# A recurrence whose new state is one scan of three elements, and a search whose sums stand inside the next count's products

## The chip, the cores and the metric

The kernel runs on one core of one Trainium2 chip. The metric is device time in microseconds, the median of several executions. Five engines work side by side and wait for each other through semaphores: PE (matrix products), DVE (elementwise, reductions, scans), ACT (activations), POOL (a second elementwise engine) and SP (which here issues transfers).

## The reference, cut to what matters

There are 4 batches of 512 rows and 512 features. Four layers are added to `x` one after the other: a top-5120 mask, attention, a GRU over the 512 rows, and a resampling. Two of them are touched:

```
# layer 0, for each batch: the 5120 largest of 512*512 values become 1, all others 0
_, idx = jax.lax.top_k(flat, k)
out = jnp.zeros((g, n * n)).at[rows, idx].set(1.0)

# layer 2: one GRU cell, 512 steps one after the other, D = 512, 4 batches
gh = h @ W_hh + b_hh
r = jax.nn.sigmoid(i_r + h_r)
z = jax.nn.sigmoid(i_z + h_z)
n = jnp.tanh(i_n + r * h_n)
h_new = (1.0 - z) * n + z * h
```

## The kernel before, in words

The program of each engine is written out by hand, in order, with explicit waits; there is no scheduler. What an engine does next is the next instruction of its own program, and it stands until that one's semaphores are reached.

**The search (layer 0).** The 5120th largest value of each batch is found bit by bit. DVE makes a 0/1 mask of 128x2048 elements (`dve_mask`; L992 for the 15 bits of the high half, L1008 and L1005 for the 16 of the low half, L998 for one count between them), PE adds the mask up with 16 matmuls against ones (`pe_count`, L1492), ACT copies the 128 partial sums (`act_search`, L557), PE adds these over the partitions with one more matmul (L1495), and ACT takes the sign of the count against a limit (`act_way`, L580) and moves the bound (`act_bound`, L591), for which the next mask of the same batch waits. The four batches take turns, so count n+4 needs the result of count n. There are 132 counts. The masks of the four batches have buffers of their own.

**The recurrence (layer 2).** The state has 512 features, 4 chunks of 128. Chunks 0 and 1 are half A, chunks 2 and 3 half B. A step on PE is twelve units (`GRU_UNITS`), each named by the half that is read, the half that is written and the gate: `AAr AAz AAn ABr BAr BAz BAn BBr ABz BBz ABn BBn`. A unit is 8 matmuls (L1790): two chunks written, two read, and two parts of the weights, high and low in fp16. The state too stands in two fp16 parts, `parts[parity][half]`, which are read as the moving operand, five copies of 4 batches x 2 parts, 40 columns. The units that read B wait for `lowB`, those that read A for `lowA`.

The result of a half goes round the engines like this. DVE adds the products of r (`dve_r_sum`, L1400) and z (`dve_z_sum`, L1407) out of PSUM into `rz`. ACT makes r (`act_sigmoid_r`, L822, into `mix`) and z (`act_sigmoid_z`, L829). DVE's scan `dve_n_line` (L1415) forms the argument of the tanh, `act_tanh` (L836) writes n into `add`. DVE makes `keep` = (1 - z) scaled (`dve_keep`, L1423), POOL makes z h (`pool_zh`, L497) into the second element of `add`. Then two scans over pairs (n, z h) with the factors (0, keep) give keep n + z h: once rounded to fp16 into `parts` (`dve_high`, L1432) and once in fp32 into `line` (`dve_line`, L1439). `dve_low` (L1448) writes the rounding error as the low part. POOL copies the line into the history (`pool_state`, L504). A scan runs along the free dimension as state = factor * state + addend, and a factor 0 starts it anew.

The order on DVE within a step is: r sum A, z sum A, n line A, r sum B, keep A, high A, line A, z sum B, low A, n line B, keep B, high B, line B, low B. Beside the steps PE has side work after the last unit, in half a group per step (`SIDE`): 8 matmuls of 128 columns for the next inputs' gates (L1723) or 4 in fp32 for output rows (L1750; 96 of the 512 steps). In the first 96 steps DVE and POOL also build the resampling table (`dve_sampling_job`, and two additions on POOL, L486 and L488, in 16 of these steps).

Of the kernel before, what the change touches and what calls it, by code (L numbers as in the profile page):

```python
# [14 lines left out]
P = 128  # L15
# [42 lines left out]
rsumA zsumA nlineA rsigA zsigA tanhA keepA zhA highA lineA lowA stateA putA  # L58
rsumB zsumB nlineB rsigB zsigB tanhB keepB zhB highB lineB lowB stateB putB
# [78 lines left out]
class Kernel:  # L138
# [39 lines left out]
    def layout(self):  # L178
# [38 lines left out]
        self.minus_h_scale = small("minus_h_scale", 1)  # L217
# [80 lines left out]
        self.parts = [[small(f"parts{parity}{half}", 2, B, 2, dtype=FP16) for half in "AB"] for parity in range(2)]  # L298
        self.rz = [small(f"rz{h}", 2, 2, B) for h in "AB"]
        self.z = [small(f"z{h}", 2, B) for h in "AB"]  # L300
# [146 lines left out]
def pool_keys(e, k, b, t):  # L447
# [3 lines left out]
    if n == 0:  # L451
        e.wait_ge(s["prepared"], 11)
# [12 lines left out]
def pool_gru(e, k):  # L465
    s = k.sem
    for half in range(2):
        e.memset(k.mix[half][:], 1.0).then_inc(s["gru_ready"], 1)
        e.memset(k.keep[half][:], 0.0).then_inc(s["gru_ready"], 1)
    e.wait_ge(s["gru_ready"], 4)  # L470
    for half in range(2):
        e.memset(k.mix[half][:, :, :, 0], 0.0).then_inc(s["gru_ready"], 1)
# [18 lines left out]
def pool_zh(e, k, st, half):  # L491
    s = k.sem
    h = "AB"[half]
    e.wait_ge(s[f"zsig{h}"], st + 1)
    if st:
        e.wait_ge(s[f"line{h}"], st)
    e.tensor_tensor(k.add[half][:, :, :, 1], k.z[half][:], k.line[half][:, :, :, 1], ALU.mult).then_inc(s[f"zh{h}"], 1)  # L497


def pool_state(e, k, st, half):  # L500
    s = k.sem
    h = "AB"[half]
    e.wait_ge(s[f"line{h}"], st + 1)
    e.tensor_copy(k.state[:, st + 1, 2 * half:2 * half + 2], k.line[half][:, :, :, 1]).then_inc(s[f"state{h}"], 1)  # L504
# [59 lines left out]
def act_way(e, k, n):  # L564
# [3 lines left out]
    count = k.bank(b, 4)[:, 2:3]  # L568
# [48 lines left out]
def act_columns(e, k, b):  # L617
    s = k.sem
    if b == 0:
        e.wait_ge(s["prepared"], 16)  # L620
# [158 lines left out]
def act_gru(e, k):  # L779
    s = k.sem  # L780
    e.wait_ge(s["hh_scale"], 7)
    unscale = act_register(e, "act_unscale", k.gate_unscale)
    e.wait_ge(s["gru_first"], 17)
# [12 lines left out]
    for st in range(S):  # L796
        q, ss = divmod(st, STEPS_PER_CHUNK)
        act_sigmoid_r(e, k, st, 0, unscale)
        act_sigmoid_z(e, k, st, 0, unscale)
# [4 lines left out]
        act_sigmoid_z(e, k, st, 1, unscale)  # L804
# [20 lines left out]
def act_sigmoid_z(e, k, st, half, unscale):  # L825
# [1010 lines left out]
```

## Time and profile before

| | |
|---|---|
| median of 3 runs | 2473.27 us (2469.03 to 2474.37) |
| the profiled execution's own time | 2475.3 us |
| its span | 2473.6 us |
| PE busy | 2243.5 us (91%) |
| weight loads of PE | 1912.7 us (77%) |
| DVE busy | 1854.6 us (75%) |
| ACT busy | 1295.0 us (52%) |
| POOL busy | 532.7 us (22%) |
| instructions | 139634 |

The span is the time from the first to the last instruction of the profiled execution; busy time is the union of an engine's instructions. Matmuls are pipelined, so their rows overlap and a busy PE need not be at its peak.

### The profile page before, as it was taken

How to read it: one execution, taken by the hardware profiler on the slowest of the kernel's cores; microseconds unless marked ns; L12 is line 12 of the kernel's file. 1: busy time of each engine (PE TensorE's matmuls, PEld its weight loads, DVE VectorE, ACT ScalarE, POOL GpSimd, SP SyncE). 2: the span in 40 equal slices, each digit the busy share in tenths (PEclk: the TensorE clock that was granted, in tenths of full speed). 3: DMA queues.
4: the chain of work that ended last, by engine and by line, in shares of the span. 5: the costliest groups of instructions: out<-in, count | busy, mean ns of one | idle time of the engine just before them, and what ended most of it. 6: DMA issues, size and time to landing. Idle time of an engine off the chain costs nothing.

```text
span 2473.6 us, 139634 instructions
## 1 busy us (share of the span) xinstructions
PE 2243.5 (91%) x58517; PEld 1912.7 (77%) x58517; DVE 1854.6 (75%) x8525; ACT 1295.0 (52%) x5693; POOL 532.7 (22%) x2223
## 2 busy tenths in 40 slices
PE   2668899898987899999999999999999999999998
PEld 2564454555544598988999999999999999999996
DVE  7876877868679588877787777777777768777775
ACT  5564856848557444444445454444444445444443
POOL 1001011020113323333222222222222222222221
PEclk9999899999999999999999999999999999999999
DMA  5000000010010000000000000000000000000000
GB/s 189 3 2 1 1 1 1 2 52 1 1 52 1 18 5 5 5 5 5 5 5 5 9 9 5 9 9 5 9 5 9 9 5 9 9 5 9 5 13 20
DMA packets 8444, 32.08 MB, mean 13 GB/s; under 512 B 836, under 2 KB 904, under 8 KB 7560
## 3 DMA queue, kind: packets, MB, share of 16 engines
q1 hardware_dynamic: 7392, 23.07, 2.5%
q8 instruction: 463, 7.59, 1.3%
q14 instruction: 165, 1.35, 0.2%
q10 hardware_dynamic: 424, 0.07, 0.0%
HBM read 18.94 MB, written 4.19 MB: 9 GB/s over the span
## 4 chain that ended last, share of the span: by engine, by line
PE 48%; DVE 9%; issue 2%; ACT 1%; POOL 1%; DVEq 0%; POOLq 0%
PE psum L1790 41%; PE psum L1723 5%; PE psum L1750 2%; DVE keepB L1423 1%; ACT mixA L822 1%; DVE nlineA L1415 1%; DVE nlineB L1415 1%; DVE rzA L1400 1%; PE psum L1472 1%; DVE keepA L1423 1%; POOL region_rows L486 1%; DVE parts1A L1432 0%; DVE parts0A L1432 0%; DVE lineA L1439 0%; DVEq L1431 0%
## 5 line engine op out<-in xcount | busy, mean ns | idle before, releaser
L1790 PE MATMUL psum<-parts0A,region_w_hh 128*128 128x40 f16 x12288 | 432.5, 179 | 16.2 <-DVE parts0A L1448 10.1
L1790 PE MATMUL psum<-parts1A,region_w_hh 128*128 128x40 f16 x12288 | 433.2, 179 | 15.3 <-DVE parts1A L1448 10.8
L1790 PE MATMUL psum<-parts1B,region_w_hh 128*128 128x40 f16 x12288 | 433.2, 179 | 7.3 <-issue 1.7
L1790 PE MATMUL psum<-parts0B,region_w_hh 128*128 128x40 f16 x12288 | 432.7, 179 | 7.4 <-DVE parts0B L1448 2.5
L822 ACT ACTIVATE mixA<-rzA 128x8 f32<-128x8 f32 x512 | 110.8, 216 | 564.3 <-DVE rzA L1400 564.1
L1790 PEld LDWEIGHTS psum<-parts0A,region_w_hh 128*128 128x128 f16 x12288 | 372.7, 96 | 25.6 <-DVE parts0A L1448 15.8
L1790 PEld LDWEIGHTS psum<-parts1A,region_w_hh 128*128 128x128 f16 x12288 | 373.3, 96 | 24.7 <-DVE parts1A L1448 16.7
L1790 PEld LDWEIGHTS psum<-parts0B,region_w_hh 128*128 128x128 f16 x12288 | 362.7, 96 | 26.2 <-DVE parts0B L1448 6.4
L1790 PEld LDWEIGHTS psum<-parts1B,region_w_hh 128*128 128x128 f16 x12288 | 362.7, 96 | 25.6 <-DVE parts1B L1448 6.0
L1400 DVE TENSOR_REDUCE rzA<-psum 128x8 f32<-128x32 f32 x512 | 97.6, 191 | 185.9 <-PE psum L1790 176.3
L497 POOL TENSOR_TENSOR addA<-zA,lineA 128x8 f32<-128x8 f32 x512 | 104.4, 204 | 586.8 <-ACT zA L829 586.8
L1723 PE MATMUL psum<-region_w_out,region_w_a 128*128 128x128 f16 x2880 | 220.1, 218 | 4.0 <-issue 3.7
L676 ACT ACTIVATE region_rows<-psum,neg_top,logit_scale 128x512 f32<-128x512 f32 x256 | 196.9, 774 | 25.6 <-DVE neg_top L1159 23.5
L744 ACT ACTIVATE psum<-region_scratch 128x24 f32<-128x24 f32 x1024 | 200.6, 196 | 0.0
L497 POOL TENSOR_TENSOR addB<-zB,lineB 128x8 f32<-128x8 f32 x512 | 104.9, 205 | 429.0 <-ACT zB L829 429.0
L829 ACT ACTIVATE zB<-rzB 128x8 f32<-128x8 f32 x512 | 106.9, 209 | 164.4 <-DVE rzB L1407 164.4
L1157 DVE TENSOR_REDUCE top<-psum 128x1 f32<-128x512 f32 x256 | 163.5, 679 | 18.7 <-PE psum L1611 18.4
L1551 PE MATMUL psum<-region_w_a,region_work 128*128 128x512 f32 x384 | 171.8, 601 | 3.5 <-ACT region_work L625 3.5
L1723 PEld LDWEIGHTS psum<-region_w_out,region_w_a 128*128 128x128 f16 x2880 | 164.0, 97 | 5.7 <-issue 5.6
L1627 PEld LDWEIGHTS psum<-ident,region_rows 128*128 128x128 f32 x1024 | 117.5, 145 | 59.7 <-issue 45.5
L1627 PE MATMUL psum<-ident,region_rows 128*128 128x128 f32 x1024 | 148.2, 284 | 16.0 <-DVE region_work L1246 12.3
L1415 DVE TENSOR_TENSOR_SCAN nlineA<-mixA,psum 128x32 f32<-128x32 f32 x512 | 113.1, 221 | 49.5 <-ACT mixA L822 7.1
(259 smaller groups left out, 4006.2 us busy)
## 6 DMA issues: line engine op xcount, KB each, us to landing
region_rows<-in_x_dram SPq DMA_DIRECT2D x4, 1024.0 KB, 12.4
out_dram<-region_w_b SPq DMA_DIRECT2D x16, 256.0 KB, 2.0
region_w_a<-in_L_cond_W_qkv_dram SPq DMA_DIRECT2D x1, 3072.0 KB, 22.7
region_w_hh<-in_L_cond_W_hh_dram SPq DMA_DIRECT2D x4, 768.0 KB, 7.2
region_rows<-in_L_cond_W_ih_dram SPq DMA_DIRECT2D x1, 3072.0 KB, 10.1
region_cond<-in_cond_dram SPq DMA_DIRECT2D x2, 1024.0 KB, 6.4
region_cols<-in_L_cond_W_emb_dram SPq DMA_DIRECT2D x1, 2048.0 KB, 18.4
region_w_out<-in_L_cond_W_out_dram SPq DMA_DIRECT2D x1, 1024.0 KB, 21.5
```

What stands on the lines that cost most here:

```text
L497: e.tensor_tensor(k.add[half][:, :, :, 1], k.z[half][:], k.line[half][:, :, :, 1], ALU.mult).then_inc(s[f"zh{h}"], 1)
L676: e.activation(k.probs[b][:, 2 * pair + i], k.bank(2 * pair + i, S), ACT.Exp, scale=k.logit_scale[:], bias=k.neg_top[:, col + i:col + i + ...
L744: e.activation(to, given, ACT.Copy).then_inc(s[f"put{h}"], 1)
L822: e.activation(k.mix[half][:, :, :, 3], k.rz[half][:, 0], ACT.Sigmoid, scale=unscale).then_inc(s[f"rsig{h}"], 1)
L829: e.activation(k.z[half][:], k.rz[half][:, 1], ACT.Sigmoid, scale=unscale).then_inc(s[f"zsig{h}"], 1)
L1157: e.tensor_reduce(k.top[:, col + i:col + i + 1], k.bank(2 * pair + i, S), AX.X, ALU.max).then_inc(s["neg_top"], 1)
L1400: e.tensor_reduce(k.rz[half][:, 0], k.slots(R_BANK[half])[:, 0], AX.X, ALU.add).then_inc(s[f"rsum{h}"], 1)
L1415: e.tensor_tensor_scan(k.nline[half][:].rearrange("p c b q -> p (c b q)"), k.mix[half][:].rearrange("p c b q -> p (c b q)"), k.bank(N_BANK ...
L1551: made = e.matmul(k.bank(bank, D), k.xnT[:, c, t * P:(t + 1) * P], k.w_qkv[:, c, i * D:(i + 1) * D], start=(c == 0), stop=(c == NC - 1))
L1627: made = e.transpose(k.bank(bank, NT, P)[:, kt], k.probs[b][:, slot, kt * P:(kt + 1) * P], k.ident[:])
L1723: made = e.matmul(k.bank(bank, P), k.w_ih16[:, part // 2, c, cols], k.x_parts[:, q % 2, part % 2, c], start=(c == part == 0), stop=(c == p ...
L1790: made = e.matmul(k.slots(bank)[:, :, ch, :, 0:2], k.w16[:, 2 * read + c, part, NC * "rzn".index(g) + 2 * half + ch], k.parts[now][read][: ...
```

## The change

Recurrence. The scans now run over three elements, (n, -h, h), with the factors (0, s, 1 - z), s being the scale of the state: n, then s n - h, then (1 - z)(s n - h) + h. `give` holds the factors. Its middle element is written once, its third by ACT each step, as the sigmoid of the negated argument (`act_give`). `line` holds the addends: tanh writes element 0, POOL writes element 1 as -1 times the new state (`pool_minus`), and element 2 is the state itself, since `dve_line` now scans in place. `keep`, `add`, `z`, `dve_keep` and `pool_zh` are gone. Element 0 of `parts` is a leftover, and PE reads elements 1 and 2 of each three.

Search. The one matmul that sums count n over the partitions stands after the tenth matmul of count n+1 (`pe_search`, `PAIRS_AHEAD = 10`), in banks of its own, 4 to 7. The embedding's products, which use bank 7, wait for the last signs.

```
-        self.keep = [small(f"keep{h}", 2, B, 2) for h in "AB"]
-        self.add = [small(f"add{h}", 2, B, 2) for h in "AB"]
-        self.line = [small(f"line{h}", 2, B, 2) for h in "AB"]
+        self.give = [small(f"give{h}", 2, B, 3) for h in "AB"]
+        self.line = [small(f"line{h}", 2, B, 3) for h in "AB"]
...
-    for st in range(S):
-        pool_zh(e, k, st, 0)
-        pool_zh(e, k, st, 1)
-        pool_state(e, k, st, 0)
-        pool_state(e, k, st, 1)
+    for st in range(S):
+        for half in range(2):
+            pool_minus(e, k, st, half)
+            pool_state(e, k, st, half)
...
+def pool_minus(e, k, st, half):
+    e.wait_ge(s[f"line{h}"], st + 1)
+    e.tensor_scalar(k.line[half][:, :, :, 1], k.line[half][:, :, :, 2], -1.0, None, ALU.mult).then_inc(s[f"minus{h}"], 1)
...
+def act_give(e, k, st, half, minus_unscale):
     e.wait_ge(s[f"zsum{h}"], st + 1)
-    e.activation(k.z[half][:], k.rz[half][:, 1], ACT.Sigmoid, scale=unscale).then_inc(s[f"zsig{h}"], 1)
+    e.activation(k.give[half][:, :, :, 2], k.rz[half][:, 1], ACT.Sigmoid, scale=minus_unscale).then_inc(s[f"give{h}"], 1)
...
 def dve_high(e, k, st, half, nxt):
     e.wait_ge(s[f"tanh{h}"], st + 1)
-    e.wait_ge(s[f"keep{h}"], st + 1)
-    e.wait_ge(s[f"zh{h}"], st + 1)
+    e.wait_ge(s[f"give{h}"], st + 1)
+    if st:
+        e.wait_ge(s[f"minus{h}"], st)
...
 def dve_line(e, k, st, half):
+    if st:
+        e.wait_ge(s[f"state{h}"], st)
+    line = k.line[half][:].rearrange("p c b q -> p (c b q)")
+    e.tensor_tensor_scan(line, k.give[half][:].rearrange("p c b q -> p (c b q)"), line, 0.0,
+                         ALU.mult, ALU.add).then_inc(s[f"line{h}"], 1)
...
-                                        k.parts[now][read][:, c].unsqueeze(1).broadcast_to([P, COPIES, B, 2]),
+                                        k.parts[now][read][:, c, :, 1:3].unsqueeze(1).broadcast_to([P, COPIES, B, 2]),
...
+def pe_search(e, k):
+    for n in range(COUNTS):
+        pe_count(e, k, n, range(PAIRS_AHEAD))
+        if n and n != FIRST_HIGH:
+            pe_sum(e, k, n - 1)
+        pe_count(e, k, n, range(PAIRS_AHEAD, PER // P))
+        if n == FIRST_HIGH - 1:
+            pe_sum(e, k, n)
+    pe_sum(e, k, COUNTS - 1)
```

On PE, in the middle of the search, the program before has, for one count after another (L1492 the mask's matmuls, L1495 the sum):

```order
L1492 MATMUL psum<-ones,region_cols 128x2 [waits mask_made]
L1492 MATMUL psum<-ones,region_cols 128x2 x15
L1495 MATMUL psum<-counts,ones 128x1 [waits sum_copied]
L1492 MATMUL psum<-ones,region_cols 128x2 [waits mask_made]
L1492 MATMUL psum<-ones,region_cols 128x2 x15
L1495 MATMUL psum<-counts,ones 128x1 [waits sum_copied]
```

In the changed program the same place on PE reads (L1503 is the sum, of the count before the one around it):

```order
L1492 MATMUL psum<-ones,region_cols 128x2 [waits sum_copied,mask_made]
L1492 MATMUL psum<-ones,region_cols 128x2 x9
L1503 MATMUL psum<-counts,ones 128x1 [waits sum_copied]
L1492 MATMUL psum<-ones,region_cols 128x2 x6
L1492 MATMUL psum<-ones,region_cols 128x2 [waits sum_copied,mask_made]
L1492 MATMUL psum<-ones,region_cols 128x2 x9
```

The sum, and with it the wait for ACT's copy, has moved from behind its own count's sixteen matmuls to behind ten of the next count's.

On DVE one step of the recurrence reads before (a scan is printed as SCALAR_TENSOR_TENSOR; the names are those of the steps above):

```order
L1400 TENSOR_REDUCE rzA<-psum 128x8 [waits r_productsA]
L1407 TENSOR_REDUCE rzA<-psum 128x8 [waits z_productsA]
L1415 SCALAR_TENSOR_TENSOR nlineA<-mixA,psum 128x32 [waits n_productsA,rsigA]
L1400 TENSOR_REDUCE rzB<-psum 128x8 [waits r_productsB]
L1423 TENSOR_SCALAR keepA<-zA,minus_h_scale 128x8 [waits zsigA]
L1432 SCALAR_TENSOR_TENSOR parts1A<-keepA,addA 128x16 [waits zhA,keepA,tanhA]
L1439 SCALAR_TENSOR_TENSOR lineA<-keepA,addA 128x16
L1407 TENSOR_REDUCE rzB<-psum 128x8 [waits z_productsB]
L1448 TENSOR_TENSOR parts1A<-lineA,parts1A 128x8 [waits highA,lineA]
L1415 SCALAR_TENSOR_TENSOR nlineB<-mixB,psum 128x32 [waits rsigB,n_productsB]
L1423 TENSOR_SCALAR keepB<-zB,minus_h_scale 128x8 [waits zsigB]
L1432 SCALAR_TENSOR_TENSOR parts1B<-keepB,addB 128x16 [waits zhB,keepB,tanhB]
```

And in the changed program:

```order
L1397 TENSOR_REDUCE rzA<-psum 128x8 [waits r_productsA]
L1404 TENSOR_REDUCE rzA<-psum 128x8 [waits z_productsA]
L1412 SCALAR_TENSOR_TENSOR nlineA<-mixA,psum 128x32 [waits n_productsA,rsigA]
L1397 TENSOR_REDUCE rzB<-psum 128x8 [waits r_productsB]
L1423 SCALAR_TENSOR_TENSOR parts1A<-giveA,lineA 128x24 [waits minusA,giveA,tanhA]
L1433 SCALAR_TENSOR_TENSOR lineA<-giveA,lineA 128x24 [waits stateA]
L1404 TENSOR_REDUCE rzB<-psum 128x8 [waits z_productsB]
L1442 TENSOR_TENSOR parts1A<-lineA,parts1A 128x8 [waits highA,lineA]
L1412 SCALAR_TENSOR_TENSOR nlineB<-mixB,psum 128x32 [waits rsigB,n_productsB]
L1423 SCALAR_TENSOR_TENSOR parts1B<-giveB,lineB 128x24 [waits minusB,giveB,tanhB]
L1433 SCALAR_TENSOR_TENSOR lineB<-giveB,lineB 128x24 [waits stateB]
```

The two keep rows are gone, the scans are of 24 elements, the high scan waits for POOL's multiplication of the step before in place of z h of the same step, and the line scan waits for POOL's copy of the step before. On POOL a step reads minus A, copy A, minus B, copy B, where it read z h A, z h B, copy A, copy B.

## Rows read from the trace of the kernel before

**Rows 1.** The page's chain of waits, by engine.

```profile
PE 48%; DVE 9%; issue 2%; ACT 1%; POOL 1%; DVEq 0%; POOLq 0%
```

**Rows 2.** Timeline in the search: start us, length us, engine, line, operation, out<-in, count.

```profile
70.05 0.17 ACT L557 ACTIVATE counts<-psum 128x1 f16<-128x1 f32 x1 [0.16 <-PE psum L1492]
70.11 0.28 ACT L591 ACTIVATE bound<-bound,way 128x1 f32<-128x1 f32 x1
...
70.28 0.19 PE L1495 MATMUL psum<-counts,ones 128*128 128x1 f16 x1 [0.27 <-ACT counts L557]
...
70.32 0.57 PE L1492 MATMUL psum<-ones,region_cols 128*128 128x2 f16 x16
70.50 0.26 ACT L580 ACTIVATE way<-psum,shift 128x1 f32<-128x1 f32 x1
70.93 0.17 ACT L557 ACTIVATE counts<-psum 128x1 f16<-128x1 f32 x1 [0.17 <-PE psum L1492]
```

**Rows 3.** Timeline of DVE, the first four masks of the high half.

```profile
40.46 2.73 DVE L992 TENSOR_SCALAR region_cols<-region_w_b,bound 128x2048 f16<-128x2048 int16 x4
```

**Rows 4.** Timeline, a mask between the halves and PE's first matmuls on it.

```profile
101.96 0.75 DVE L998 TENSOR_SCALAR region_cols<-region_w_b,above 128x2048 f16<-128x2048 int16 x1
...
102.77 0.29 PE L1492 MATMUL psum<-ones,region_cols 128*128 128x2 f16 x5 [2.08 <-DVE region_cols L998]
```

**Rows 5.** Timeline of one step without side work, DVE, ACT and POOL.

```profile
2429.34 0.19 DVE L1400 TENSOR_REDUCE rzA<-psum 128x8 f32<-128x32 f32 x1 [0.46 <-PE psum L1790]
...
2429.57 0.22 ACT L822 ACTIVATE mixA<-rzA 128x8 f32<-128x8 f32 x1 [1.21 <-DVE rzA L1400]
...
2429.81 0.22 DVE L1415 TENSOR_TENSOR_SCAN nlineA<-mixA,psum 128x32 f32<-128x32 f32 x1
...
2430.05 0.23 DVE L1423 TENSOR_SCALAR keepA<-zA,minus_h_scale 128x8 f32<-128x8 f32 x1
...
2430.07 0.22 ACT L836 ACTIVATE addA<-nlineA 128x8 f32<-128x8 f32 x1
...
2430.39 0.19 DVE L1432 TENSOR_TENSOR_SCAN parts1A<-keepA,addA 128x16 f16<-128x16 f32 x1
...
2430.70 0.17 DVE L1448 TENSOR_TENSOR parts1A<-lineA,parts1A 128x8 f16<-128x8 f32 x1
...
2430.79 0.22 DVE L1415 TENSOR_TENSOR_SCAN nlineB<-mixB,psum 128x32 f32<-128x32 f32 x1
...
2431.04 0.22 ACT L836 ACTIVATE addB<-nlineB 128x8 f32<-128x8 f32 x1
...
2431.40 0.19 DVE L1432 TENSOR_TENSOR_SCAN parts1B<-keepB,addB 128x16 f16<-128x16 f32 x1
...
2431.72 0.17 DVE L1448 TENSOR_TENSOR parts1B<-lineB,parts1B 128x8 f16<-128x8 f32 x1
2431.74 0.20 POOL L504 COPY region_work<-lineB 128x8 f32<-128x8 f32 x1 [0.34 <-DVE lineB L1439]
...
2432.35 0.19 DVE L1400 TENSOR_REDUCE rzA<-psum 128x8 f32<-128x32 f32 x1 [0.46 <-PE psum L1790]
```

**Rows 6.** Timeline of PE: side work for output rows, then for gates.

```profile
1410.71 0.69 PE L1750 MATMUL psum<-region_rows,region_cols 128*128 128x128 f32 x4
...
1413.51 0.35 PE L1790 MATMUL psum<-parts0B,region_w_hh 128*128 128x40 f16 x8
1413.71 0.61 PE L1723 MATMUL psum<-region_w_out,region_w_a 128*128 128x128 f16 x8
1414.16 0.96 PE L1790 MATMUL psum<-parts1A,region_w_hh 128*128 128x40 f16 x32
```

**Rows 7.** Groups by line, a scan of 512: shapes, count | busy us, mean ns | idle before.

```profile
L1045 DVE TENSOR_TENSOR_SCAN region_w_hh<-region_w_hh,zero 128x512 f32<-128x512 f16 x16 | 19.4, 1215 | 0.0
```

**Rows 8.** Groups by line of DVE between 1200 and 1500 us.

```profile
L1400 DVE TENSOR_REDUCE rzA<-psum 128x8 f32<-128x32 f32 x98 | 18.8, 192 | 37.5 <-PE psum L1790 35.4
```

**Rows 9.** Groups by line, high A in steps of one parity.

```profile
L1432 DVE TENSOR_TENSOR_SCAN parts1A<-keepA,addA 128x16 f16<-128x16 f32 x256 | 49.1, 192 | 31.9 <-POOL addA L497 5.2 <-DVE keepA L1423 0.9 <-ACT addA L836 0.5
```

More of the change, by code:

```diff
@@ L468, in pool_gru @@
         e.memset(k.mix[half][:], 1.0).then_inc(s["gru_ready"], 1)
-        e.memset(k.keep[half][:], 0.0).then_inc(s["gru_ready"], 1)
+        e.memset(k.give[half][:], 0.0).then_inc(s["gru_ready"], 1)
     e.wait_ge(s["gru_ready"], 4)
+    e.wait_ge(s["prepared"], 9)
     for half in range(2):
+        e.tensor_copy(k.give[half][:, :, :, 1], k.h_scale[:].unsqueeze(2).broadcast_to([P, 2, B])).then_inc(s["gru_ready"], 1)
         e.memset(k.mix[half][:, :, :, 0], 0.0).then_inc(s["gru_ready"], 1)
@@ L503, in pool_state @@
     e.wait_ge(s[f"line{h}"], st + 1)
[L504 removed]
+    e.tensor_copy(k.state[:, st + 1, 2 * half:2 * half + 2], k.line[half][:, :, :, 2]).then_inc(s[f"state{h}"], 1)
 def act_program(e, k):
@@ L567, in act_way @@
     col = slice(b, b + 1)
-    count = k.bank(b, 4)[:, 2:3]
+    count = k.bank(4 + b, 4)[:, 2:3]
     if kind == "sign":
@@ L835, in act_tanh @@
     e.wait_ge(s[f"nline{h}"], st + 1)
-    e.activation(k.add[half][:, :, :, 0], k.nline[half][:, :, :, 3], ACT.Tanh, scale=unscale).then_inc(s[f"tanh{h}"], 1)
+    e.activation(k.line[half][:, :, :, 0], k.nline[half][:, :, :, 3], ACT.Tanh, scale=unscale).then_inc(s[f"tanh{h}"], 1)
 def dve_program(e, k):
@@ L1429, in dve_high @@
     e.wait_ge(s[f"tanh{h}"], st + 1)
-    e.wait_ge(s[f"keep{h}"], st + 1)
-    e.wait_ge(s[f"zh{h}"], st + 1)
-    e.tensor_tensor_scan(k.parts[nxt][half][:].rearrange("p c b q -> p (c b q)"), k.keep[half][:].rearrange("p c b q -> p (c b q)"),
-                         k.add[half][:].rearrange("p c b q -> p (c b q)"), 0.0, ALU.mult, ALU.add).then_inc(s[f"high{h}"], 1)
+    e.wait_ge(s[f"give{h}"], st + 1)
+    if st:
+        e.wait_ge(s[f"minus{h}"], st)
+    e.tensor_tensor_scan(k.parts[nxt][half][:].rearrange("p c b q -> p (c b q)"), k.give[half][:].rearrange("p c b q -> p (c b q)"),
+                         k.line[half][:].rearrange("p c b q -> p (c b q)"), 0.0, ALU.mult, ALU.add).then_inc(s[f"high{h}"], 1)
 def dve_line(e, k, st, half):
@@ L1438, in dve_line @@
     h = "AB"[half]
-    e.tensor_tensor_scan(k.line[half][:].rearrange("p c b q -> p (c b q)"), k.keep[half][:].rearrange("p c b q -> p (c b q)"),
-                         k.add[half][:].rearrange("p c b q -> p (c b q)"), 0.0, ALU.mult, ALU.add).then_inc(s[f"line{h}"], 1)
+    if st:
[3 more added lines that the diff above has]
+                         ALU.mult, ALU.add).then_inc(s[f"line{h}"], 1)
 def dve_low(e, k, st, half, nxt):
@@ L1447, in dve_low @@
     e.wait_ge(s[f"high{h}"], st + 1)
-    e.tensor_tensor(k.parts[nxt][half][:, :, :, 0], k.line[half][:, :, :, 1], k.parts[nxt][half][:, :, :, 1],
+    e.tensor_tensor(k.parts[nxt][half][:, :, :, 1], k.line[half][:, :, :, 2], k.parts[nxt][half][:, :, :, 2],
                     ALU.subtract).then_inc(s[f"low{h}"], 1)
@@ L1456, in pe_program @@
     e.transpose(k.bank(7, VEC_ROWS), k.vec_rows, k.ident[0:VEC_ROWS, 0:VEC_ROWS]).then_inc(s["vec"], 1)
-    for n in range(COUNTS):
-        pe_count(e, k, n)
+    pe_search(e, k)
     pe_embed(e, k)
```

81 lines of the change are left out of this document (40 added, 41 removed).

## The prediction

> **What bounds the kernel now.** I read the chain of waits first [rows 1]: it lays 48% of the span on PE and almost nothing on the others, so it says that the products of the recurrence set the pace. The timeline of single steps says otherwise, and I go by it. The recurrence runs from 862 us to the end, 512 steps; in 300 us of it there are 98 of them, a mean of 3.06 us, and DVE's first sum waits 35.4 of these us for PE [rows 8]. A step's products alone are 96 matmuls. Eight of them take from 1413.51 to 1413.71 [rows 6], 0.025 us each, so 2.41 us with the unrounded spacing (the rows' spacing gives 2.40), and the side work of most steps (8 matmuls of 128 columns) takes 0.45 us more, from 1413.71 to 1414.16. That is 2.86 us. The step of [rows 5] has no side work, 2.41 us of PE, and still lasts 2432.35 - 2429.34 = 3.01 us. So the pace is not PE's but that of a ring, which the reader can follow in [rows 5]: r sum A 2429.34, sigmoid (mixA), n line A, tanh A (the L836 row), high A (L1432), line A (a scan like high, without a row here), low A (L1448), n line B, tanh B, high B, low B, and 0.63 us later, over B's first eight matmuls, r sum A again. PE shows as busy because a matmul's row is far longer than the spacing of two; in a step with side work 3.01 - 2.86 = 0.15 us is all that PE waits.
>
> Before that stands the search for the 5120th value, 132 counts. Its rows [rows 2] repeat every 70.93 - 70.05 = 0.88 us. DVE makes a mask in less when nothing holds it: four in 2.73 us [rows 3], and a mask's row is 0.75 us (the first row of [rows 4]), so (2.73 - 0.75)/3 = 0.66 us from mask to mask. The 0.88 us are PE's: 16 matmuls until ACT's copy (70.32 to 70.93, 0.61), copy to sum 0.23, sum to the next count 0.04. PE stands idle while ACT copies.
>
> **The search.** PE's sum of count n moves behind the first ten matmuls of count n+1. PE's own work per count is then at most 0.57 us (the row of 16) and 0.04 for the sum, and nothing in it waits if the copy is done: the copy ends 0.61 + 0.17 = 0.78 us after the count's first matmul, and the sum is due at 0.66 + 0.27 = 0.93. What is late next is DVE, or the ring through the bound of the same batch four counts later. From the start of a mask: to PE's first matmul 0.81 [rows 4], next count 0.66, ten matmuls 0.27, sum to sign 0.22 [rows 2], the sign itself 0.26 and 0.03 to the bound, the bound itself 0.28 [rows 2], 0.03 to DVE (the 0.03 are what n line A shows below): 2.56 us. Four masks take 4 x 0.66 = 2.64 us. DVE stays the bound, by 0.08 us. Of the 132 counts, 56 of the high and 60 of the low half run at 0.88 us today (the first four of the high half are those of [rows 3]; the four counts between are held by a DVE instruction of 2.35 us and stay). Gain: 116 x (0.88 - 0.66) = 25.5 us. At the end the embedding's products now wait for the last sign, some 0.4 us by the rows above (sum to sign, sign), which I charge: -25.1. If the ring rather than DVE binds at 0.70, the gain is 21.
>
> **The recurrence, part by part.** Per half, DVE loses keep and POOL loses z h; POOL gains a multiplication by -1 right after each line, off the ring (it is used a step later), and ACT's second sigmoid writes 1 - z, same form and count. The scans grow from 16 to 24 elements.
> What goes: keep A starts 2430.05 and ends 2430.28, a hair before tanh A ends (2430.07 + 0.22 = 2430.29), and high A starts only 2430.39, because two of its waits (z h, keep) end in an instruction of their own ahead of it. A scan whose last wait is for ACT starts sooner: n line A at 2429.81 follows mix A's end at 2429.57 + 0.22 = 2429.79, 0.02 to 0.03 us. In the new form the waits for give and minus are over long before tanh, so high A comes 0.03 behind tanh A, at 2430.32: -0.07. On B tanh ends 2431.04 + 0.22 = 2431.26 and high starts 2431.40; it would start 2431.29: -0.11. Together -0.18.
> What comes: a scan of 512 elements takes 1215 ns and n line, of 32, takes 220 [rows 5, 7], (1215 - 220)/480 = 2.07 ns an element, so 8 more cost 0.0166 us. High and line of each half stand in the ring: 4 x 0.0166 = +0.066. The bounds of this price are 0 (if the fixed part hides them) and +0.13 (twice the slope); I take the slope.
> Net -0.114 us: a ring of 2.90 us. PE needs 2.86, so in steps with gate work the ring still just decides. Steps with output rows (4 fp32 matmuls, 96 of 512 steps) cost PE 0.69 - 0.61 = 0.08 more [rows 6], near 2.95, so there only 0.06 is gained. N line B also waits for its own products, PE's last eight of the step, so a faster A would not bring more. Sum: 416 x 0.114 = 47.4, 96 x 0.06 = 5.8.
> Of the moved POOL work: z h of A was behind POOL's additions for the sampling table in 16 of the first 96 steps. The profile charges high A 5.2 us of waiting for it in the steps of one parity [rows 9], and those of the other have as many. With z h gone nothing urgent stands behind those additions; of some 10 us I take -8.
> What is given back: a mean step is 3.06, a smooth one 3.01, so 0.05 x 512 = 26 us are hiccups, part of them on PE, beside those that PE's 0.15 us of slack a step swallowed. Now it has 0.04. I charge +10 (0 to 20).
> On the port: POOL's copy of line B starts at 2431.74, just behind low B at 2431.72 [rows 5], and low B takes 0.17 us beside it as low A does alone; the new multiplication takes that place, behind A too. I cost it at nothing, because low A starts first; if POOL came first, see below.
> The moving operand of the products is now pairs with a gap of one element, 8 columns over 24 bytes and not 16. Such an operand is not in the trace. Bounds: a 128-column matmul takes 0.45/8 = 0.056 us, so 40 columns need 0.0175 of the 0.025 us that pass anyway; up to 1.4 times the column time costs nothing, twice costs 0.010 each. Below nothing is excluded, as the columns are hidden already. I take 0.
> The Trainium skill (SBUF — State Buffer, in the note on cachelines under "Door 1: The DMA port swizzle") says that reads run at full bandwidth with two or more hits per 16-byte line, and that each step to a new line pays. The new pattern has two or more hits a line but twice as many lines. No row here shows it; by the first half of the rule the price is nothing, by the second it is the slow rival below.
>
> **Sum.** Against the profiled execution, 2475.3 us (span 2473.6; the median of the three runs is 2 us lower): -25.1 - 47.4 - 5.8 - 8 + 10 = -76.3, so 2399 us.
>
> **The rivals.**
> (1) PE becomes the pace. For: the chain of waits [rows 1] and a slack of 0.04. PE's waits for A's sums, its put and its own fetches then add up, and the step goes to about 2.97. Against: its 32 matmuls of [rows 6] take 0.96 us, 31 spacings and one matmul's length, so no hole. Price: 0.06 of the step's gain lost, 512 x 0.06 = 31 us: 2430.
> (2) High still starts 0.10 behind tanh, since three waits remain on it. Then A gains nothing, B 0.04, the scans cost 0.066: +0.03 a step, +14 us, and with the search 2475 + 14 - 25 = 2464. Against: n line A has two waits and comes 0.03 behind the last.
> (3) The search does not close at 0.66 but stays at 0.88, since ACT takes the next copy only behind the sign: 2399 + 25 = 2424. For: copy, sign and bound take 0.17 + 0.26 + 0.28 = 0.71 us by their rows, more than 0.66. Against: the rows overlap, the bound starts at 70.11 and the copy ahead of it ends at 70.22.
> (4) Slower: the gapped moving operand. It decides from 0.025 us a matmul on; at twice the column time, 0.035 us, PE needs 3.36 + 0.45 = 3.81 a step, 0.75 above today's mean: 2475 - 25 + 384, about 2834. Against: the 0.0075 us of cover. The port pair works the same way at a lower price: if POOL's product by -1 held up both low parts for its 0.2 us, the step would be 2.90 + 0.40 = 3.30, 0.24 above today's mean, near 2475 - 25 + 123 = 2573.
> The Trainium skill (SBUF — State Buffer, "Who interferes with whom") states that a DVE instruction with two SBUF inputs and a GpSimd read exclude each other. Copy B beside low B does not show it; by that rule the new operation would wait for low, not low for it, so the sum stays.
>
> **How the numbers follow.** Main case 0.60, its own range 2380 to 2415 (scan price, hiccups 0 to 20, sampling 0 to 12, search 21 to 25). Rival 1 0.16, rival 2 0.10, rival 3 0.07, rival 4 with the port 0.07. Range 2378 to 2450: it holds the main case nearly whole, rivals 1 and 3. A measurement of this kernel can tell about 0.2% from no change, 5 us. Faster is all but rival 4: 0.91, a remainder near nothing change 0.02, slower 0.07.
>
> **What would show it.** Right: masks every 0.66 us and PE's sum without idle time before it; high 0.03 us behind tanh; steps at 2.90, with rows at 2.95; matmuls still every 0.025 us; the scans 17 ns longer; no wait of high for POOL. Wrong: matmuls further apart, a high that waits for minus or give, a low that waits for POOL, holes in PE's runs of 32, or masks at more than 0.7 us.

## The result, and the profile after

| | before | after |
|---|---|---|
| median | 2473.82 us (2469.03 to 2474.37, 4 runs) | 2432.26 us (2425.71 to 2434.5, 4 runs) |
| profiled execution, its span | 2475.3 us, 2473.6 us | 2434.5 us, 2432.7 us |
| first r sum A of the recurrence | 862.55 us | 837.05 us |
| from there to the last r sum A (511 steps) | 1588.1 us | 1571.2 us |
| instructions | 139634 | 137723 |

The change makes the kernel 41.6 us faster: the ratio is 0.9832, 95% interval 0.9809 to 0.9855. The forecast was 2399, with a range of 2378 to 2450, so the gain is little over half of the 76 us forecast. The search brings the 25 us that were expected; the recurrence brings 17 where 51 were expected (47.4 + 5.8 + 8 - 10).

**The search.** Timeline of ACT and of PE in the search, in the columns of [rows 2]; L1503 is the sum over the partitions:

```profile
60.30 0.26 ACT L577 ACTIVATE way<-psum,shift 128x1 f32<-128x1 f32 x1
60.46 0.17 ACT L554 ACTIVATE counts<-psum 128x1 f16<-128x1 f32 x1
60.59 0.30 ACT L588 ACTIVATE bound<-bound,way 128x1 f32<-128x1 f32 x1
60.96 0.26 ACT L577 ACTIVATE way<-psum,shift 128x1 f32<-128x1 f32 x1
61.12 0.17 ACT L554 ACTIVATE counts<-psum 128x1 f16<-128x1 f32 x1
61.25 0.29 ACT L588 ACTIVATE bound<-bound,way 128x1 f32<-128x1 f32 x1
```

```profile
60.76 0.17 PE L1503 MATMUL psum<-counts,ones 128*128 128x1 f16 x1
60.78 0.78 PE L1492 MATMUL psum<-ones,region_cols 128*128 128x2 f16 x16
61.42 0.17 PE L1503 MATMUL psum<-counts,ones 128*128 128x1 f16 x1
```

A count now takes 61.42 - 60.76 = 0.66 us instead of 0.88, and no row has idle time in brackets. DVE's masks follow each other without a hole. This row, the first ten masks of the high half, gives (6.71 - 0.75)/9 = 0.66 us from mask to mask, the pace that [rows 3] had for four:

```profile
40.45 6.71 DVE L990 TENSOR_SCALAR region_cols<-region_w_b,bound 128x2048 f16<-128x2048 int16 x10
```

**A step without side work.** Timeline of DVE, ACT and POOL, to be laid beside [rows 5] (lineA from L834 is the tanh, from L1433 the new state, from L494 the product by -1):

```profile
2390.53 0.19 DVE L1397 TENSOR_REDUCE rzA<-psum 128x8 f32<-128x32 f32 x1 [0.46 <-PE psum L1809]
...
2391.26 0.22 ACT L834 ACTIVATE lineA<-nlineA 128x8 f32<-128x8 f32 x1
...
2391.51 0.21 DVE L1423 TENSOR_TENSOR_SCAN parts0A<-giveA,lineA 128x24 f16<-128x24 f32 x1 [0.19 <-ACT lineA L834]
...
2391.64 0.18 DVE L1433 TENSOR_TENSOR_SCAN lineA<-giveA,lineA 128x24 f32<-128x24 f32 x1
...
2391.85 0.17 DVE L1442 TENSOR_TENSOR parts0A<-lineA,parts0A 128x8 f16<-128x8 f32 x1
2391.91 0.24 POOL L494 TENSOR_SCALAR lineA<-lineA 128x8 f32<-128x8 f32 x1 [1.59 <-DVE lineA L1433]
...
2392.19 0.22 ACT L834 ACTIVATE lineB<-nlineB 128x8 f32<-128x8 f32 x1
...
2392.44 0.21 DVE L1423 TENSOR_TENSOR_SCAN parts0B<-giveB,lineB 128x24 f16<-128x24 f32 x1 [0.28 <-ACT lineB L834]
...
2392.78 0.18 DVE L1442 TENSOR_TENSOR parts0B<-lineB,parts0B 128x8 f16<-128x8 f32 x1
...
2393.43 0.19 DVE L1397 TENSOR_REDUCE rzA<-psum 128x8 f32<-128x32 f32 x1 [0.47 <-PE psum L1809]
```

The step takes 2393.43 - 2390.53 = 2.90 us, as forecast, against 3.01. High A starts 0.03 us behind the end of tanh A (2391.48), high B 0.03 behind tanh B (2392.41). So the ring did what was said of it. All that is missing is in the steps that are not smooth: the mean step is 3.075 us, 0.18 above the smooth one, where before it was 3.108, 0.10 above. Steps with gate work are smooth at the same 2.90 us: of the 360, the 155 in which PE has no hole (the word is explained below) take 2.90 in the median, the 205 with one 3.19 in the mean. So PE's 2.86 us of work did not take over as the pace; what comes on top of it did.

**Where the rest went.** Timeline of PE in two steps with gate work (L1809 are the products, L1742 the gate work):

```profile
1542.81 0.70 PE L1809 MATMUL psum<-parts1A,region_w_hh 128*128 128x40 f16 x21
1543.79 0.48 PE L1809 MATMUL psum<-parts1A,region_w_hh 128*128 128x40 f16 x11 [0.28 <-issue]
1544.11 0.95 PE L1809 MATMUL psum<-parts1B,region_w_hh 128*128 128x40 f16 x32
...
1545.71 0.61 PE L1742 MATMUL psum<-region_w_out,region_w_a 128*128 128x128 f16 x8
1546.16 0.96 PE L1809 MATMUL psum<-parts0A,region_w_hh 128*128 128x40 f16 x32
1546.98 0.45 PE L1809 MATMUL psum<-parts0B,region_w_hh 128*128 128x40 f16 x11
1547.71 0.69 PE L1809 MATMUL psum<-parts0B,region_w_hh 128*128 128x40 f16 x21 [0.28 <-issue]
```

Compare the first matmul of each row with the next. A run of 32 on one operand is cut after 21 matmuls, and later one after 11. Neither matmul behind the cut waits for a semaphore; the bracket says "issue", nothing that the profile shows. From 1542.81 to 1543.79 are 0.98 us for 21 matmuls that take 0.53: PE lost 0.46 us there (before the cut the pipeline still drains, so the bracket shows only 0.28 of them).

PE's own view of it, the waits between 1000 and 2300 us (engine, line, what ended the idle time: us in all, times, longest), of before:

```profile
DVE rzA L1400 <- PE psum L1790: 148.0, 319, 1.1
PEld psum L1790 <- issue: 16.5, 61, 0.6
```

and of after:

```profile
DVE rzA L1397 <- PE psum L1809: 177.3, 337, 1.1
PEld psum L1809 <- issue: 41.8, 129, 0.7
```

DVE's first sum of a step waits longer for PE than before (177.3 against 148.0 us), though its ring is shorter, and PE's weight loads (PEld) stand 41.8 us without a semaphore to wait for, against 16.5.

I call a hole, from here on, a matmul of the recurrence that waits for no semaphore and starts over 45 ns later behind the last one than is usual for that kind of matmul, and count what it is late. Over the whole recurrence before has 227 holes with 40.8 us, after has 339 with 79.5 us: 38.7 us more. Of these, 94 before and 95 after are another thing: one of the three distances between the four fp32 matmuls of an output-row step is 80 ns longer than the other two, in every kernel here, 8 us in all. They cancel in every difference below, but 8 us of each sum of holes are theirs. Lateness of matmuls that do wait for a semaphore fell from 105 to 42 us. The smooth step brings 511 x 0.11 = 56 us, the holes take 39 back, and 17 is what is measured. (The sum is rougher than it looks: the 96 steps with output rows gain 0.06 and not 0.11, which is 5 us less, and the sampling below brings about 5 more.)

**What the holes are.** Of the 216 distances between neighbouring larger holes (over 0.1 us, under 1500 matmuls apart) all lie within 3 matmuls of a multiple of 127. A matmul is two instructions, the load of its weights and the product, and PE has about two waits a step in instructions of their own: 127 matmuls and two waits are 256 instructions. The page's list of DMA queues (packets, MB, share) has a row that fits, the same in both kernels:

```profile
q8 instruction: 463, 7.59, 1.3%
```

Each of these 463 packets is 16,384 bytes. Counting PE's instructions makes the tie exact. The trace has 118,633 of them (118,504 before), weight loads, matmuls and waits, and a 256th of that is 463.4 (462.9). Numbered in the order of the program, all 218 larger holes of after, and all 103 of before, fall on one place, instruction 193 or 194 of each 256. In the recurrence a packet starts every 3.8 us in the mean (one of after 3.23 us behind the last, all others 3.3 or more) and mostly takes 0.88 to 1.4 us, 1.1 in the median. The 3.8 is the rate at which PE uses blocks, its waits included, and not by itself a limit of the supply. Theory "code": q8 carries PE's program in blocks of 256 instructions, a hole is PE standing at the start of a block that has not come, and the old kernel hid most of that time in the waits for its slower ring. The rival, "columns": PE's own 2.86 us of work and its waits add up, whatever the code.

### The profile page after: what moved, and what is told of

Same layout as the page of the kernel before. It is cut to its first block, busy times and chain, and to the rows that moved or that the text cites. A ratio compares the mean times of both kernels' runs of the same rounds, so it can differ in the third digit from the quotient of the medians.

```text
span 2432.7 us, 137723 instructions
## 1 busy us (share of the span) xinstructions
PE 2221.6 (91%) x58517; PEld 1910.9 (79%) x58517; DVE 1675.5 (69%) x7503; ACT 1299.2 (53%) x5693; POOL 563.4 (23%) x2225
## 4 chain that ended last, share of the span: by engine, by line
PE 74%; DVE 16%; issue 5%; ACT 4%; DMA 0%; POOL 0%; ACTq 0%; DVEq 0%; POOLq 0%
PE psum L1809 49%; PE psum L1742 7%; PE psum L1570 5%; DVE top L1155 3%; PE psum L1610 2%; PE psum L1646 2%; PE psum L1769 2%; PE psum L1664 2%; DVE region_cols L1006 2%; DVE region_cols L990 2%; DVE region_work L1244 1%; PE psum L1630 1%; PE psum L1589 1%; ACT region_rows L673 1%; PE psum L1548 1%
## 5 line engine op out<-in xcount | busy, mean ns | idle before, releaser
L1809 PE MATMUL psum<-parts0A,region_w_hh 128*128 128x40 f16 x12288 | 436.3, 182 | 16.5 <-DVE parts0A L1442 6.9
L1809 PE MATMUL psum<-parts1A,region_w_hh 128*128 128x40 f16 x12288 | 436.7, 182 | 16.0 <-issue 7.5
L1809 PE MATMUL psum<-parts0B,region_w_hh 128*128 128x40 f16 x12288 | 441.5, 182 | 8.7 <-issue 7.6
L1809 PE MATMUL psum<-parts1B,region_w_hh 128*128 128x40 f16 x12288 | 437.3, 182 | 10.2 <-issue 8.0
L1809 PEld LDWEIGHTS psum<-parts0A,region_w_hh 128*128 128x128 f16 x12288 | 374.9, 96 | 25.4 <-issue 13.2
L1809 PEld LDWEIGHTS psum<-parts1A,region_w_hh 128*128 128x128 f16 x12288 | 374.3, 96 | 25.8 <-issue 13.0
L1809 PEld LDWEIGHTS psum<-parts0B,region_w_hh 128*128 128x128 f16 x12288 | 367.6, 96 | 15.8 <-issue 11.1
L1809 PEld LDWEIGHTS psum<-parts1B,region_w_hh 128*128 128x128 f16 x12288 | 364.5, 96 | 18.7 <-issue 12.6
L494 POOL TENSOR_SCALAR lineA<-lineA 128x8 f32<-128x8 f32 x512 | 122.2, 239 | 837.9 <-DVE lineA L1433 837.9
L1742 PE MATMUL psum<-region_w_out,region_w_a 128*128 128x128 f16 x2880 | 221.2, 218 | 4.9 <-issue 4.5
L494 POOL TENSOR_SCALAR lineB<-lineB 128x8 f32<-128x8 f32 x512 | 130.2, 254 | 312.7 <-DVE lineB L1433 312.7
L827 ACT ACTIVATE giveB<-rzB 128x8 f32<-128x8 f32 x512 | 109.1, 213 | 132.7 <-DVE rzB L1404 130.8
L1742 PEld LDWEIGHTS psum<-region_w_out,region_w_a 128*128 128x128 f16 x2880 | 164.1, 97 | 7.4 <-issue 7.3
```

The costliest lines, as they stand in the source:

```text
L494: e.tensor_scalar(k.line[half][:, :, :, 1], k.line[half][:, :, :, 2], -1.0, None, ALU.mult).then_inc(s[f"minus{h}"], 1)
L827: e.activation(k.give[half][:, :, :, 2], k.rz[half][:, 1], ACT.Sigmoid, scale=minus_unscale).then_inc(s[f"give{h}"], 1)
L1742: made = e.matmul(k.bank(bank, P), k.w_ih16[:, part // 2, c, cols], k.x_parts[:, q % 2, part % 2, c], start=(c == part == 0), stop=(c == p ...
L1809: made = e.matmul(k.slots(bank)[:, :, ch, :, 0:2], k.w16[:, 2 * read + c, part, NC * "rzn".index(g) + 2 * half + ch], k.parts[now][read][: ...
```

## The experiments

Each kernel ran beside runs of the kernel before on the same chip, whose median was 2468 to 2480 us from chip to chip; so ratios are compared, and "in us" is ratio x 2474. Spans, step times and holes are those of the one profiled execution of each kernel. The expectations for the operand and for the merged matmuls leave out the 8 us of fp32 holes; the sums given under "Measured" have them in.

**The two parts by themselves.** Search alone (the diff is the change's own in `pe_count`, `pe_sum`, `pe_search`, `pe_embed` and the two bank numbers):

> The kernel before with the change's search alone (PE's sum of count n behind ten matmuls of count n+1, the sums' own banks); the recurrence stays the old one. The trace after has a mask every 0.66 us and starts the recurrence 25.5 us earlier, so all theories expect about -25 us: 2449 us (2446 to 2451). It fixes what the recurrence is charged with: the rest of the -41 us, some -16. If instead it measures -35 or more, the new recurrence is worth nothing by itself.

Measured: 2449.75 us, 0.9904 (0.9889 to 0.9919), -24 us. The recurrence alone (the same lines undone in the changed kernel):

> The changed kernel with the old search: the recurrence's change alone. With the search alone at -24 us and both at -41, all that is left if the two parts add is -17: 2457 us (2453 to 2461), holes without a wait near 80 us as in the changed kernel. The prediction's sum for this part was -51 (2423). If it is under 2445, the two parts cost each other something, for instance by where the blocks of code fall.

Measured: 2459.66 us, 0.9934 (0.9910 to 0.9957), -16 us, and 79.3 us of holes. The parts add: 24 + 16 = 40 of 41.6. The recurrence is what fell short.

**The operand.**

```diff
-        self.parts = [[small(f"parts{parity}{half}", 2, B, 2, dtype=FP16) for half in "AB"] for parity in range(2)]
+        self.parts = [[(small(f"parts0{half}", 2, B, 2, 2, dtype=FP16) if parity == 0 else view("work", 32.0625 + at / 16, FP16, 2, B, 2, 2))[:, :, :, :, 0]
+                       for at, half in enumerate("AB")] for parity in range(2)]
```

> The kernel before with one change: the 16-bit parts of the state lie four bytes apart, so that PE's moving operand reads 8 columns over 32 bytes with a hole beside each (the change itself has 24 bytes and a hole beside each pair). Theory 'code' (PE's instruction stream arrives in blocks of 16 KB, 256 instructions, and a PE without slack waits for a block): the operand is innocent, 2474 us as before, within 5, with some 140 holes over 45 ns in PE's runs and some 32 us in them. Rival 'operand' (the gap makes the holes): the number of holes rises to about 250 and 70 us, and the time by some 10 to 40 us, since the old ring has only 0.15 us of slack a step.

Measured: 2477.48 us, 1.0015 (1.0003 to 1.0027), +4 us, with 182 holes of 28 us (87 of 20 us without the fp32 ones), fewer than before. Matmuls still follow every 25 ns. So the operand makes no holes. The 4 us may be in the ring: the median step is 3.017 us against 3.010, and x 511 that is 3.6 us. That is not shown: the profiled execution took 2470.39 us, and its whole recurrence is 5 us shorter than before's (1583.1 against 1588.1).

**Instructions against columns.** Four kernels change only the matmuls of gate work (L1742), in 360 of the 512 steps. First with the same columns:

```diff
-            for part in range(4):
-                made = e.matmul(k.bank(bank, P), k.w_ih16[:, part // 2, c, cols], k.x_parts[:, q % 2, part % 2, c],
-                                start=(c == part == 0), stop=(c == part == NC - 1))
+            for part in range(2):
+                made = e.matmul(k.bank(bank, 2, P), k.w_ih16[:, part, c, cols], k.x_parts[:, q % 2, :, c],
+                                start=(c == part == 0), stop=(c == NC - 1 and part == 1))
```

This kernel leaves the products with the low part of x out of its result: PE makes them, into 128 sums of their own.

> The changed kernel, in which the side work on the input gates is issued as 4 matmuls of 256 columns a step instead of 8 of 128 (the same stationary block, both parts of x as one moving operand; the second 128 sums are left out of the result). PE's columns are the same, its instructions in the 360 steps with gate work fall from 210 to 202. 'Code': a block of 256 instructions costs about 3.4 to 3.8 us to arrive, 14 ns each, so those steps fall from 3.08 toward 2.95: -30 us (-15 to -50), about 2402 us, and the holes from 72 us to under 45. 'Columns' (rival 1 as it was put: PE's own work of 2.86 us and its waits add up): no change, 2432 within 5.

Measured: 2402.29 us, 0.9699 (0.9684 to 0.9714): 33 us less than the changed kernel, with PE's columns untouched. Holes 264 with 48.5 us (40.8 without the fp32 ones; under 45 was expected). The packets of q8 are 452, 11 fewer: 360 x 8 = 2880 instructions are 11.25 blocks of 256. That too ties q8 to PE's program. Now half the columns and all the instructions:

```diff
-                made = e.matmul(k.bank(bank, P), k.w_ih16[:, part // 2, c, cols], k.x_parts[:, q % 2, part % 2, c],
+                made = e.matmul(k.bank(bank, P)[:, :P // 2], k.w_ih16[:, part // 2, c, cols], k.x_parts[:, q % 2, part % 2, c, :P // 2],
                                 start=(c == part == 0), stop=(c == part == NC - 1))
```

> The changed kernel, in which each of the 8 matmuls of gate work a step has 64 columns instead of 128 (half of the gate inputs are left out). Instructions as in the changed kernel, PE's columns 0.22 us less in 360 steps. 'Columns': PE has 0.26 us of slack against the ring of 2.90 again and the steps with gate work fall from 3.08 to 2.92: -50 to -60 us, about 2377. 'Code': blocks are taken just as fast as before, at 210 instructions a step: at most -20 us, 2412 to 2432, and the holes stay or grow.

Measured: 2437.2 us, 0.9851 (0.9835 to 0.9867). A fifth of a microsecond of PE's work less in 360 steps brings nothing. Its waits between 1000 and 2300 us:

```profile
PEld psum L1809 <- issue: 51.7, 145, 0.8
```

By the matmuls' own distances PE saved 360 x 8 x 26 ns = 75 us. Of these, 5 went into the holes (84.9 us of them against 79.5) and 73 into matmuls that wait for a semaphore (115 us late against 42). Steps without a hole still take 2.90 us, since the ring is their pace, and the holes cost what they cost before. Then the opposite, the same columns in more instructions:

```diff
-                made = e.matmul(k.bank(bank, P), k.w_ih16[:, part // 2, c, cols], k.x_parts[:, q % 2, part % 2, c],
-                                start=(c == part == 0), stop=(c == part == NC - 1))
+                for at in (0, P // 2):
+                    made = e.matmul(k.bank(bank, P)[:, at:at + P // 2], k.w_ih16[:, part // 2, c, cols],
+                                    k.x_parts[:, q % 2, part % 2, c, at:at + P // 2],
+                                    start=(c == part == at == 0), stop=(c == part == NC - 1), ...)
```

> The changed kernel, in which each of the 8 matmuls of gate work is issued as two of 64 columns on the same stationary block. PE's columns are the same (64 columns take 0.028 us, over the 0.025 from matmul to matmul, by the run with half the columns), its instructions in 360 steps rise from 210 to 226. 'Code': 16 instructions of some 14 ns are 0.22 us more in each such step, of which little is hidden: +50 to +85 us, about 2500 us, with the holes over 120 us. 'Columns': no change, 2432 to 2438.

Measured: 2509.56 us, 1.0120 (1.0089 to 1.0151), in us 71 above the changed kernel and slower than before. That is 71/(360 x 16) = 12 ns an instruction. Of the page and of the waits in the same stretch:

```profile
q8 instruction: 486, 7.96, 1.4%
```

```profile
PEld psum L1811 <- issue: 85.7, 185, 0.8
```

23 packets more for 5760 instructions (22.5 blocks), and 415 holes with 146.4 us. They keep their distance of 127 matmuls (303 of 304), though a step now has 112 and not 104, and all 305 larger ones stand again on instruction 193 or 194 of a block: the holes go by the count of instructions, not by a place in the step. Each matmul added brings a weight load too, so one may ask whether the loads by themselves cost the time. They do not: two matmuls of 64 columns follow each other in 2 x 29 ns where one of 128 took 55, which is 9 us in all, and the other 67 of the 76 us by which the profiled recurrence is longer (1646.8 against 1571.2) are holes at the blocks' borders.

The last corner has the instructions of the merged kernel and the columns of the halved one (the high part of x alone, `part in range(2)`, against both parts of the weights):

> The changed kernel with the high part of x alone against both parts of W_ih: 4 matmuls of 128 columns a step (x's low part is left out of the gate inputs, as it is left out of the result in the run with merged matmuls). Instructions as in the merged run, 202, and PE's columns 0.22 us fewer. 'Code': as merged, 2402, or a few us less (2392 to 2404), since a block then has to last 256 instructions whatever the columns. 'Columns', on top of code: another -20 or more, 2380.

Measured: 2398.06 us, 0.9676 (0.9653 to 0.9699), holes 45.3 us. Its waits:

```profile
PEld psum L1809 <- issue: 23.3, 86, 0.6
```

Laid beside the halved kernel it is the cleanest pair: 512 columns of gate work a step in both, as 8 matmuls 0.9851, as 4 matmuls 0.9676. Eight instructions a step are 43 us (34 by the spans of the two recurrences, 1569.7 and 1535.6, with holes of 84.9 and 45.3). Between them, 6 matmuls (only the product of the two low parts left out, `part in range(3)`):

> The changed kernel without the product of the low part of W_ih and the low part of x: 6 matmuls of 128 columns a step instead of 8, 206 instructions instead of 210, PE's columns 0.11 us less. 'Code': half of what the merging gave by its 8 instructions, some -15 us, and nothing for the columns: 2417 (2408 to 2425).

Measured: 2414.59 us, 0.9737 (0.9716 to 0.9757), in us 23 less than the changed kernel, where 15 were expected (by the profiled recurrences 15 less, 1556.5 against 1571.2, 9 of them holes).

**The same on the old ring.**

> The kernel before with the gate work as 4 matmuls of 256 columns (the second 128 sums left out of the result). The same edit gave 30 us on the changed kernel. 'Code': the old ring of 3.01 us leaves PE slack in which most blocks arrive unseen, the holes of before sum to 41 us, and about half of them go: 2474 - 15 = 2459 (2450 to 2466), so the edit is worth half of what it is on the new ring, and the recurrence's change on this base is worth more than without it: from 2459 - 25 to 2402 is some 32 us against 16. Rival 'merging is good by itself, whatever the ring': the same 30 us, 2444.

Measured: 2460.93 us, 0.9926 (0.9908 to 0.9945): -18 us, holes 18.7 us (11.3 without the fp32 ones). So fewer instructions are worth 18 us on the old ring and 33 on the new one.

**Code nearly out of the way.** One matmul of gate work in every second step:

```diff
-            for part in range(4):
-                made = e.matmul(k.bank(bank, P), k.w_ih16[:, part // 2, c, cols], k.x_parts[:, q % 2, part % 2, c],
-                                start=(c == part == 0), stop=(c == part == NC - 1))
+            if c == NC - 1:
+                made = e.matmul(k.bank(bank, P), k.w_ih16[:, 0, c, cols], k.x_parts[:, q % 2, 0, c], start=True, stop=True)
```

> The changed kernel with one matmul of gate work in every second such step (the gate inputs of all chunks but the first are left out but for one product): 195 instructions a step on average in all of the 360 steps. From 226, 210, 206 and 202 instructions the times were 2510, 2432, 2415 and 2398 to 2402: 13 ns an instruction and then less. 'Code': it goes on flattening toward the ring's 2.90 us a step: 2380 (2368 to 2392). If PE's code is no longer felt at all, every smooth step is 2.90 and only the other hiccups stay: about 2365.

> The kernel before with the same cut of gate work. 'Code': with PE's blocks out of the way the new ring is worth what the steps say, 0.11 us x 511 = 56 us, beside the search's 24; so this one stands 65 to 80 us above the changed kernel with the same cut, about 2452 (2445 to 2460), where the two kernels as they are stand 41 apart. 'The rest of the gain is lost elsewhere' (DVE's or ACT's own code, queues): the distance stays 41 to 50, about 2425.

Measured: 2386.35 us, 0.9679 (0.9665 to 0.9693), and 2459.52 us, 0.9967 (0.9954 to 0.9980). By its ratio the first is no better than the kernel with 202 instructions (0.9676); by the profiled executions its recurrence is 11 us shorter (1524.2 against 1535.6), with 11 us less of holes. The two ran on different chips, whose medians of before are 2480 and 2468, so how far the curve still falls below 202 instructions is not settled. The distance of the two is 0.0288, 71 us, inside the 65 to 80 of "code", and with the search's 24 taken off the new ring is worth 47.

| gate work, columns x matmuls | instructions in such a step | time, new ring | holes, us | old ring | the ring's change alone |
|---|---|---|---|---|---|
| 16 x 64 | 226 | 1.0120 | 146 | | |
| 8 x 128 (as it is) | 210 | 0.9832 | 80 | 1 | -18 us |
| 8 x 64 | 210 | 0.9851 | 85 | | |
| 6 x 128 | 206 | 0.9737 | 70 | | |
| 4 x 256 | 202 | 0.9699 | 49 | 0.9926 | -32 us |
| 4 x 128 | 202 | 0.9676 | 45 | | |
| hardly any | 195 | 0.9679 | 35 | 0.9967 | -47 us |

The last column is the new ring's ratio less the old ring's, x 2474, plus the 24 us of the search. The old ring's holes are 41, 19 and 17 us. About 8 us of every sum of holes are the fp32 ones. The old ring's 0.9926 and 0.9967 are from different chips as well; their profiled executions, 1572.6 and 1569.8 us of recurrence, stand the other way round. The distances in the last column come out the same from the spans: 2457.8 - 2401.6 - 24 = 32 and 2455.7 - 2384.6 - 24 = 47.

**The best version.** The high part of x alone, and DVE's instructions for the low part gone too:

> The changed kernel with the gate inputs from the high part of x alone (4 matmuls of 128 columns a step), and with DVE's 60 instructions that make the low part gone too. Against 2398 with them: each took 0.3 us or so of DVE in four steps of each chunk, part of it in the ring: -2 to -8 us, 2393.

Measured: 2388.58 us, 0.9670 (0.9656 to 0.9683). It beats both kernels, by 3.3% and 1.6%, at the price of gate inputs without the low part of x; against 0.9676 with DVE's instructions in place the difference is within the intervals, so that part is not shown to bring anything. Who wants to keep the low part of x has 0.9737 with 6 matmuls.

## Why the prediction was right, and where it was wrong

The range holds the measured time, but the main case (2399, its own range 2380 to 2415) misses it by 33 us. The range reached so far up because of rival 1, whose price turned out right and whose mechanism only in part; to that extent it is luck.

**The search: right.** 116 x 0.22 = 25.5 us forecast, the recurrence starts 25.5 us earlier; by itself it measures 24. Rival 3 is out.

**The smooth step: right.** 0.11 us a step forecast and found, with gate work or without. The scans' price was taken from a slope, 17 ns each. By the groups over all 512 steps high went from 192 ns [rows 9] to 208 to 210 and line from 168 to 182. High's mean, of after, with what ended its waits:

```profile
L1423 DVE TENSOR_TENSOR_SCAN parts1A<-giveA,lineA 128x24 f16<-128x24 f32 x256 | 53.8, 210 | 44.7 <-ACT lineA L834 44.2
```

No wait of high is charged to POOL any more. Rival 2 (high still 0.10 behind tanh) is out.

**The operand and the port: right to cost them at nothing.** The matmuls follow every 25 ns, and low A is 177 to 178 ns beside POOL's product, where low had 170 to 171: 7 ns, not 0.2 us. Rival 4 is out in both its forms.

**Steps with output rows: right.** The quickest are 2.93 us, and those without a further hole 2.945 in the median; 2.95 was forecast.

**Sampling: too high.** The first 96 steps became 7.2 us shorter, the other 415 9.7 us, 0.023 a step. But the first 96 also have 8.7 us more of holes than before (13.2 against 4.5), so without them they gained 15.9, of which 96 x 0.11 = 10.6 are the smooth step's. Some 5 us belong to what only they have; 8 was forecast. POOL's rows of waiting, 5.2 and 5.3 us, are gone.

**The hiccups: the step that failed.** The prediction said "a mean step is 3.06, a smooth one 3.01, so 0.05 x 512 = 26 us are hiccups, part of them on PE [...]. Now it has 0.04. I charge +10 (0 to 20)." Measured: 50 us before (the stretch that I had read was the quieter one), 90 after, so +40 are given back, twice the upper bound. The term was sized by what hiccups there were and not by what they were. The slack of 0.15 us a step was taken for a cushion against odd events; it was time in which PE's next block of code came. The demand could have been read from the trace before: PE runs through 256 instructions in 25 ns x 127 = 3.2 us (3.5 with gate work) when nothing holds it, packets start 3.8 us apart, and 103 larger holes already stand at the blocks' borders. Four comparisons show that it is instructions and not columns: same columns and 8 instructions a step fewer, -33 us; same instructions and half the columns, +5; same columns and 16 more, +71; and the pair of 512 columns, 43 us apart. With the code nearly out of the way the ring is worth 47 us, where the forecast had 47.4 + 5.8 + 8 = 61 before hiccups, and the new ring there still has 18 us more of holes (35 against 17).

**Rival 1** was put at 2430, which is where the kernel is, for "PE's waits for A's sums, its put and its own fetches". One of its three causes holds: the fetches. Waits for semaphores on PE became shorter. Nor did the step go to about 2.97 throughout: it is 2.90 without a hole and 3.19 with one. The argument against it, a run of 32 matmuls without a hole [rows 6], was one run, and at one block in 127 matmuls most runs have no border in them. It had a chance of 0.16 and deserved more.

The Trainium skill (Runtime: NRT & Kernel Launch, "Instruction fetch mechanics") describes a fifo refilled in blocks of 16 KiB, 256 instructions, and calls the cost of crossing into the next one "mostly hidden". The size agrees with the packets of 16,384 bytes and the 127 matmuls. That it is hidden nearly holds for the old ring with merged gate work (19 us of holes in 1573) and not here: 80 us in the changed kernel, 146 with 226 instructions a step.

**What stays open.** Why a block comes late is shown only as far as times go. Between one border and the next exactly one packet starts, in all 412 cases of the recurrence, before and after; so nothing shows PE's code coming more than one block ahead. For the 246 borders of after with a hole the medians are 1.2 us from the border before to the packet's start, 1.2 us for the packet and 1.4 us from its end to the matmul behind the hole (1.25 to 1.56 at the 5th and 95th percentile), 3.86 us in all. PE needs 3.2 to 3.5 us for the 256 instructions. This reads like a loop of its own, in which the next packet is asked for at a border, but that it is asked for there is not shown, nor what the 1.2 and the 1.4 us consist of. The 364 steps of the best version without such a hole are together 16 us longer than 2.90 each; their cause was not tried. The second queue of instructions (q14: 165 packets before, 149 after) fits the other engines' instructions, 21130 and 19090, at 128 a packet (165.1 and 149.1); whether it ever holds one of them up was not tried.

## What to carry to other kernels

- Where an engine issues one short instruction after the other for long, count its program as a resource: here PE runs through a block of 256 instructions in 3.2 to 3.5 us, and where it had to wait for the next one 3.86 us passed from border to border. Slack at a semaphore is then not free time, and shortening another engine's ring returns only what the code allows.
- Cuts in the middle of a run, at matmuls that wait for nothing and at equal distances in instructions, are the sign. The remedy is fewer, wider instructions: 256 columns in one matmul instead of two of 128 gave twice the gain of the change's own recurrence. As it was run, that kernel left the second 128 sums out of its result; what adding them back would cost was not tried.
- When a mean is above the smooth case, find what the difference consists of before sizing how much slack it needs.

## What the runs showed of the hardware that was not expected

- PE's program comes over a queue of its own in packets of 16,384 bytes. Without the fp32 ones PE stands 0.29 us in the mean at a hole (72 us in 244), and up to 0.7 by the row of its waits. Between two borders of blocks there is exactly one packet.
- Half the columns of the gate work (64 for 128, 29 ns from matmul to matmul for 55) moved the time by less than its interval. Halving the matmuls at equal columns (4 x 128 for 8 x 64) moved it by 1.8%.
- A scan on DVE whose third wait had long been met still started 0.10 us behind tanh in the old kernel [rows 5] and starts 0.03 behind it in the new one, which has three waits too. So the number of waits alone does not cost it. An explanation that fits, and that no run tested, is how shortly before they are met: keep A ended 0.01 us ahead of tanh A there, give and minus are over long before here.
